# A hybrid eight-layer kernel: the begin of relative attention in another order, projections and adapter products inside the ends of its calls

## The reference

```python
# relative attention, 16 heads of 8
qx, kx, vx = split_head(x @ Wq.T), split_head(x @ Wk.T), split_head(x @ Wv.T)
srel = srel_skew(jnp.einsum('bhnd,hmd->bhnm', qx, ex))       # ex: rel_embed by head
qk = (jnp.einsum('bhnd,bhmd->bhnm', qx, kx) + srel) * inv_dim
atten = jax.nn.softmax(qk - mask, axis=-1)                   # causal
out = jnp.einsum('bhnm,bhmd->bhnd', atten, vx)...
return out @ Wp.T + bp
# adapter layer: 8 experts of width 64, two chosen by sequence
gate = jax.nn.softmax(x.mean(axis=1) @ gate_w.T); top_w, top_i = top_k(gate, 2)
h = gelu(x @ Wd + bd) * top_w;  out = h @ Wu + top_w * bu
```

## Time and profile before

| | |
|---|---|
| median of the 3 timed runs | 3797.18 us (3792.64 to 3798.52) |
| the profiled execution, its own time | 3799.16 us |
| its span | 3797.1 us |
| TensorE busy | 3561.5 us, 94% |
| VectorE busy | 2288.1 us, 60% |
| ScalarE busy | 1731.8 us, 46% |
| GpSimd busy | 822.9 us, 22% |
| mean granted TensorE clock | 0.992 |

### The profile page before, as it was taken

How to read it: one execution, slowest core, us unless ns; L and a number is a source line. 1 busy time by engine, 2 the same in 40 slices (tenths; PEclk the granted TensorE clock), 3 DMA queues, 4 the chain that set the end, 5 groups by cost and what they waited for, 6 DMA issues and landing times.

```text
span 3797.1 us, 78536 instructions
## 1 busy us (share of the span) xinstructions
PE 3561.5 (94%) x31023; PEld 2402.4 (63%) x31023; DVE 2288.1 (60%) x7482; ACT 1731.8 (46%) x3542; POOL 822.9 (22%) x1374
## 2 busy tenths in 40 slices
PE   6999999988999999998899999998889999999888
PEld 3666667666565667766556556776665656677665
DVE  4546455677554655567755554567776555456766
ACT  2425333466442523356644252335565335233556
POOL 3202023411210302332021030333302112033330
PEclk8999999999999999999999999999999999999999
DMA  3000000000000000000000000000000000000000
GB/s 89 2 1 2 1 1 1 2 2 2 13 1 1 2 1 1 1 2 2 1 13 1 1 2 1 1 1 2 2 7 8 1 1 1 1 1 1 2 2 9
DMA packets 27032, 17.47 MB, mean 5 GB/s; under 512 B 9425, under 2 KB 26274, under 8 KB 26658
## 3 DMA queue, kind: packets, MB, share of 16 engines
q1 hardware_dynamic: 26658, 12.32, 1.2%
HBM read 10.22 MB, written 2.10 MB: 3 GB/s over the span
## 4 chain that ended last, share of the span: by engine, by line
PE 69%; DVE 11%; POOL 7%; ACT 6%; issue 5%; SPq 1%; DVEq 0%; another core or an unknown queue 0%; POOLq 0%
PE banks L1252 9%; PE banks L1219 8%; PE banks L1214 8%; PE banks L1064 5%; PE banks L1103 5%; POOL work L563 5%; PE banks L1118 4%; PE banks L1043 3%; PE banks L1306 3%; PE banks L1538 3%; ACT work L887 2%; ACT work L881 2%; PE banks L1373 2%; PE banks L1551 2%; DVE work L2034 2%
## 5 line engine op out<-in xcount | busy, mean ns | idle before, releaser
L1723 DVE CUSTOM_DVE_ANT_0 work<-banks,mask_row 128x512 f32<-128x512 f32 (+3 forms) x1024 | 433.9, 486 | 276.1 <-PE banks L1064 276.0
L718 ACT ACTIVATE work<-banks 128x512 f32<-128x512 f32 x352 | 209.3, 597 | 654.1 <-PE banks L1214 638.9
L1814 DVE TENSOR_TENSOR work<-work,banks 128x512 f32<-128x512 f32 x352 | 242.0, 688 | 426.5 <-PE banks L1219 404.6
L519 POOL TENSOR_TENSOR rstd<-rstd,half 128x4 f32<-128x4 f32 x65 | 65.6, 1009 | 1933.9 <-DVE rstd L1647 1933.9
L741 ACT ACTIVATE work<-banks 128x384 f32<-128x384 f32 (+1 forms) x768 | 358.8, 534 | 255.2 <-PE banks L1103 254.7
L1103 PE MATMUL banks<-work 32*128 32x512 f32 (+3 forms) x2048 | 443.8, 464 | 6.5 <-DVE work L1723 3.9
L1252 PEld LDWEIGHTS banks<-wd,work 128*128 128x128 f32 (+2 forms) x4096 | 355.0, 189 | 135.3 <-issue 131.4
L1064 PE MATMUL banks<-work 32*128 32x384 f32 (+3 forms) x2048 | 406.1, 457 | 11.9 <-ACT work L727 6.4
L1252 PE MATMUL banks<-wd,work 128*128 128x128 f32 (+2 forms) x4096 | 365.8, 278 | 0.0
L530 POOL TENSOR_SCALAR_AFFINE_SELECT work<-work 128x128 f32<-128x128 f32 (+1 forms) x768 | 253.4, 333 | 460.8 <-ACT work L741 437.5
L1103 PEld LDWEIGHTS banks<-work 32*128 32x128 f32 x2048 | 243.0, 183 | 77.2 <-ACT work L741 39.4
(11 more groups left out here) (320 smaller groups left out, 6596.6 us busy)
## 6 DMA issues: line engine op xcount, KB each, us to landing
x_a<-in_L_attn_a_x_dram SPq DMA_DIRECT2D x5, 256.0 KB, 2.8
x_b<-in_L_attn_a_x_dram SPq DMA_DIRECT2D x4, 256.0 KB, 3.0
wg<-in_L_ffn_Wg_dram SPq DMA_DIRECT2D x2, 512.0 KB
wu<-in_L_ffn_Wu_dram SPq DMA_DIRECT2D x2, 512.0 KB
wd<-in_L_ffn_Wd_dram SPq DMA_DIRECT2D x16, 64.0 KB
out_dram<-x_a SPq DMA_DIRECT2D x4, 256.0 KB, 2.5
out_dram<-x_b SPq DMA_DIRECT2D x4, 256.0 KB, 2.6
wk_l<-in_L_attn_a_Wk_dram SPq DMA_DIRECT2D x1, 512.0 KB, 4.1
```

The costliest lines, as they stand in the source:

```text
L1723: m = eng.tensor_tensor_reduce(out=summed[:, k % 2, col:col + N], in0=bank(bk)[:, col:col + N], in1=mask_row[:, T - N:T], scale=1.0, scala ...
```

## The change

Nothing is added to or taken from what is computed; two fill products fewer are issued in a turn. It has six edits.

1. The rest of q goes to `xn` of the same sequence (free by then), the rest of k to its own place (`res_k`), so the buffer of mask step 0 no longer overlaps them. VectorE's order becomes: rest of q, mask(0) high, rest of k, mask(0) middle, low of q, low of k, values, mask(1), and both copies of stacked k.
2. GpSimd's mask(1) waits for VectorE's two instructions of mask(0) (`r_qm`) in place of both low parts.
3. TensorE does round 0 of the relative products before the first two spreads; these and round 1 follow, behind a wait for the values.
4. b's projection, and ScalarE's high parts for it, move from the start of b's relative call into the end of a's, behind the last `weigh`; the output transposes go to bank 6. a's sum into x on VectorE moves behind b's low parts.
5. The third adapter call's gate product (bank 3) and four down products move into the end of b's relative call, around the last head group and in the place of the two fills of `pe_out`.
6. In the adapters the gate product stands behind two tiles of up products instead of three; before the relative calls `pe_norm` stands behind two tiles of the second call's instead of four. The first sums of scores wait for the selects of their own blocks instead of for all of them.

```diff
@@ part(...) of relative attention
-        res, at = part(ring_at, [2, T])
-        k_parts, at = part(at, [3, T], BF16)
+        k_parts, _ = part(ring_at + 2 * T, [3, T], BF16)
+        res_k, _ = part(ring_at + 2 * T + 3 * T // 2, [T])
@@ pool_rel, mask(c)
                 if c == 1:
-                    eng.wait_ge(r_shift, n + 1)
-                    eng.wait_ge(a_lo, 2 * n + 2)
+                    eng.wait_ge(r_qm, 12 * n + 2)
@@ end of act_rel
-            if n == 1:
+            if n == 0:
+                act_first_parts(eng, 1, float(HD) ** -0.5)
+            else:
                 gate_exp(eng, 2)
@@ pe_adapters
-            up(n, (0, 1, 2))
+            up(n, (0, 1))
             eng.wait_ge(xnT_ok, adapter_call(n + 1))
             gate_products(eng, n + 1, 7)
-            up(n, (3,))
+            up(n, (2, 3))
...
-            up(n + 1, (0, 1, 2, 3))
+            up(n + 1, (0, 1))
+            if n == 0:
+                pe_norm(eng, adapter_call(n + 1) + 1, 0)
+            up(n + 1, (2, 3))
@@ pe_rel, begin
             eng.wait_ge(a_res, 2 * n + 2)
-            eng.wait_ge(a_v, 4 + n + 1)
-            pe_spread(eng, n, 0)
-            pe_spread(eng, n, 1)
             for i in range(P // 8):
+                if i == 1:
+                    eng.wait_ge(a_v, 4 + n + 1)
+                    pe_spread(eng, n, 0)
+                    pe_spread(eng, n, 1)
@@ pe_rel, end
             weigh(NG - 1)
-            if n == 1:
-                gate_products(eng, 2, 1)
-            group_rows(eng, n, NG * (5 + n) - 1, 7)
-            pe_out(eng, 4 + n, rel_call(n), w[:, 3, :], bp_row, 0, lambda: fill(eng, 3, 2))
+            if n == 0:
+                pe_project(eng, 1, w)
+            else:
+                gate_products(eng, 2, 3)
+                adapter_down(eng, 2, 0)
+            group_rows(eng, n, NG * (5 + n) - 1, 7)
+            if n == 1:
+                adapter_down(eng, 2, 1)
+                adapter_down(eng, 2, 2)
+            pe_out(eng, 4 + n, rel_call(n), w[:, 3, :], bp_row, 6,
+                   lambda: fill(eng, 3, 2) if n == 0 else adapter_down(eng, 2, 3))
@@ rel on VectorE, begin
+                first_rest(0)
+                eng.wait_ge(r_shift, n + 1)
+                mask_q(eng, 0, 0).then_inc(r_qm, 1)
+                first_rest(1)
+                eng.wait_ge(a_mid, 2 * n + 1)
+                mask_q(eng, 0, 1).then_inc(r_qm, 1)
+                last_part(0)
+                last_part(1)
+                if n == 1:
+                    add_to_x(4, a_y, 4)
+                eng.wait_ge(a_proj, 3 * n + 3)
+                copy_values(2)
+                eng.wait_ge(a_lo, 2 * n + 2)
+                mask(1)
                 stack_k(n, 0)
-                mask(1)
                 stack_k(n, 1)
...
-                eng.wait_ge(r_diag, 4 * (P // IC) * n + 4 * (P // IC))
...
+                    if p == 0:
+                        eng.wait_ge(r_diag, 4 * (P // IC) * (n + 1) - (3, 1, 0)[j])
```

More of the change, by code:

```diff
@@ L685, in act_norm, with rest, act_first_parts @@
             eng.activation(xnTs[j % 2][:, :], bank(bk), ACT.Copy).then_inc(xnT_ok, 1)
-        def act_parts(eng, n, scale):
+        def rest(n, w):
+            return (xns[n][:, :, :].rearrange("p t d -> p (t d)"), res_k)[w]
+        def act_first_parts(eng, n, scale):
             eng.wait_ge(a_proj, 3 * n + 1)
@@ L691, in act_parts @@
             eng.activation(qk_part(1, 0), bank(1), ACT.Copy).then_inc(a_hi, 1)
+        def act_parts(eng, n):
             for w in range(2):
                 eng.wait_ge(a_res, 2 * n + w + 1)
-                eng.activation(qk_part(w, 1), res[:, w, :], ACT.Copy).then_inc(a_mid, 1)
+                eng.activation(qk_part(w, 1), rest(n, w), ACT.Copy).then_inc(a_mid, 1)
         def act_stack(eng, n, w, at):
@@ L1419, in gate_products, with adapter_down @@
             eng.matmul(bank(bk)[:, 0:E], gates[n // 2]["rep"], gateT[:, :], start=True, stop=True).then_inc(d_gate_ok, 1)
+        def adapter_down(eng, m, k):
+            if k == 0:
+                eng.wait_ge(xnT_ok, adapter_call(m))
+            if m == 2 and k == 3:
+                eng.wait_ge(d_lgs, m + 1)
+            eng.matmul(bank(k), downT[:, k, :], xnTs[m % 2][:, :], start=True, stop=True).then_inc(d_dn, 1)
         def pe_adapters(eng, n):
             def down(m):
-                eng.wait_ge(xnT_ok, adapter_call(m))
                 for k in range(KD):
-                    if m == 2 and k == 1:
-                        eng.wait_ge(d_lgs, m + 1)
-                    eng.matmul(bank(k), downT[:, k, :], xnTs[m % 2][:, :], start=True, stop=True).then_inc(d_dn, 1)
+                    adapter_down(eng, m, k)
             def mix_column(m):
@@ L1447, in up @@
                     i.then_inc(d_y, 1)
-            down(n)
+            if n == 0:
+                down(n)
             mix_column(n)
@@ L1667, in copy_values @@
                    .then_inc(a_v, 1)
-            def parts_of_qk(n, scale):
-                for w in range(2):
-                    eng.wait_ge(a_hi, 2 * n + w + 1)
-                    eng.scalar_tensor_tensor(out=res[:, w, :], in0=bank(w), scalar=(scale, 1.0)[w],
-                                             in1=qk_part(w, 0), op0=ALU.mult,
-                                             op1=ALU.subtract).then_inc(a_res, 1)
-                eng.memset(q_parts[:, 0:2, 0:1], 0.0).then_inc(r_shift, 1)
-                for w in range(2):
-                    eng.wait_ge(a_res, 2 * n + w + 1)
-                    eng.wait_ge(a_mid, 2 * n + w + 1)
-                    eng.tensor_tensor(qk_part(w, 2), res[:, w, :], qk_part(w, 1),
-                                      ALU.subtract).then_inc(a_lo, 1)
-                eng.wait_ge(a_proj, 3 * n + 3)
-                copy_values(2)
             def stack_k(n, at):
@@ L1998, in rel, with first_rest, last_part @@
             def rel(n):
-                parts_of_qk(n, float(HD) ** -0.5)
+                def first_rest(w):
+                    eng.wait_ge(a_hi, 2 * n + w + 1)
+                    eng.scalar_tensor_tensor(out=rest(n, w), in0=bank(w), scalar=(float(HD) ** -0.5, 1.0)[w],
+                                             in1=qk_part(w, 0), op0=ALU.mult,
+                                             op1=ALU.subtract).then_inc(a_res, 1)
+                def last_part(w):
+                    eng.wait_ge(a_res, 2 * n + w + 1)
+                    eng.wait_ge(a_mid, 2 * n + w + 1)
+                    eng.tensor_tensor(qk_part(w, 2), rest(n, w), qk_part(w, 1),
+                                      ALU.subtract).then_inc(a_lo, 1)
                 def mask(c):
-                    if c == 0:
-                        eng.wait_ge(r_shift, n + 1)
-                        eng.wait_ge(a_lo, 2 * n + 2)
                     if c >= 2:
```

23 lines of the change are left out of this document (15 added, 8 removed).

## The result

| | before | changed |
|---|---|---|
| median of the runs | 3792.2 us (12 runs, 3786.7 to 3800.4) | 3803.6 us (12 runs, 3797.6 to 3811.0) |
| ratio, 95% interval | | 1.0030 (1.0022 to 1.0039) |
| span of the profiled execution | 3797.1 us | 3804.4 us |
| mean granted clock | 0.992 | 0.988 |

The changed kernel is **slower by 0.3%**; 3793.5 us and "the same" had been forecast, with a range up to 3800. Both intervals lie above 1, so the change makes the kernel slower; by how much, 0.1 or 0.3%, differs between the two series.

What follows compares the result with a forecast made beforehand. TensorE (69% of the chain) was taken as the bound, GpSimd as second limit in the loop. +0.1 - 0.8 - 0.26 = -0.95 us a turn, -3.8 us in four, gave 3795.4, as median 3793.5 us; range 3776 to 3800.

Steps and rivals of the forecast that it cites:

- Adapters into a's call: Adapter calls ahead of a's relative call: the norm two tiles before the end starts a's projection 0.8 us earlier.
- Begin of a's call: Reordered steps before a's selects: low part of k held up beside GpSimd's mask, selects 0.65 us later.
- the higher of two bounds: Low part of k on VectorE beside GpSimd's mask(1): between 0.6 and 2.6 us, taken as 2.6.
- Loop's end: End of a's loop follows GpSimd's chain, 0.65 us later, less 0.58 us of TensorE idle time: +0.1 us.
- the split wait: Loop's end: first sum goes after the first of the last four selects, 1.4 us sooner, removing 0.58 us TensorE idle.
- b's call: b's relative call: selects 0.55 us earlier and 0.23 us of idle time gone, -0.8 us.
- End of b's call: Into the third adapter call: early down products gain nothing and cost 0.7 us; gate product 0.26 us sooner.
- Sum without the clock: Whole kernel: -0.95 us a turn, -3.8 us over four turns.
- rival 3: Three new TensorE idle stretches a turn could drop its clock, 1.7 us each; all 12 give 3814 us; chance 0.08.
- one counterexample: End of a turn, TensorE waiting for rows of xn_a: 1.56 us idle left the clock at full, cited against rival 3.
- Rival 1: Begin of both relative calls: low part of k isn't held up, values 2.0 us earlier, -4.8 us a turn, 3778; chance 0.17.
- Rival 2: Loop: GpSimd's chain has slack and the end follows TensorE, -2.3 us a turn, 3788 us; chance 0.12.

Runs made afterwards that it cites:

- e3: Changed kernel with one wait more: GpSimd's mask(1) waits for both low parts again, early down products left in; 3781.6 us, ratio 0.9961 to before.
- e2: Changed kernel with 15 fills instead of 6 in front of the third adapter norm; 3792.6 us, ratio 0.9991 to before.
- r2: Changed kernel with 11 fills instead of 6 in front of the third adapter norm; 3791.7 us, ratio 0.9989 to before.
- r1: Changed kernel run once more, unedited, for a second trace; 3799.3 us, ratio 1.0011 to before.
- e5: Changed kernel with 8 fills instead of 6 in front of the third adapter norm; 3799.6 us, ratio 1.0012 to before.
- e6: Kernel before with only the adapter calls' new order (gate product one tile ahead, norm of a's call two tiles ahead); 3785.6 us, ratio 0.9980.
- e4: Changed kernel with down products back behind b's output projection and GpSimd's mask(1) waiting for both low parts; 3774.4 us, ratio 0.9945 to before.
- e8: e4 with rounds 0 and 1 both ahead of the first spreads; 3768.2 us, ratio 0.9931 to before.
- e1: Changed kernel with the third adapter call's down products back behind b's output projection, gate product still early; 3782.5 us, ratio 0.9966 to before.
- e7: e4 with b's projection put back at the begin of b's call; 3779.3 us, ratio 0.9961 to before.

## Why the prediction was wrong

By its own steps:

- **Adapters into a's call**, -0.8 us: measured -0.86 us. Right.
- **Begin of a's call.** The low part of k at 2.6 us, the higher of two bounds: 2.52 us. TensorE idle 1.99 us in front of the spreads (2.3 forecast). Selects 14.35 us after the projection forecast, 14.23 us measured. The rule of the Trainium skill, SBUF — State Buffer, section "Who interferes with whom", by which the higher bound was to hold, agrees here: where the two engines overlap, whichever instruction started second is held up. The low part of q started first and took its 0.69 us, GpSimd's mask then took 2.42 instead of 2.03 us, and the low part of k, behind it, 2.52 us; in e3, with nothing beside it, 0.69 us.
- **Loop's end.** +0.1 us for a's call forecast; it is 1.34 - 0.86 - 0.67 = -0.19 us. The stage behind the first scores, where the split wait was to gain 0.58 us, is 0.67 us shorter (no run isolates that wait), and the selects were later by 0.44 us, not 0.65 us.
- **b's call**, -0.8 us: -0.95 - 0.31 = -1.26 us.
- **End of b's call.** The early down products delay x_b and gain nothing: rows of `xn_b` 10.16 us after the last weigh instead of 9.12 us, TensorE idle 1.98 us (2.1 forecast). With the clock at full (e2, r2) the gate product comes at 14.56 us, 0.09 us sooner than before, for 0.26 us forecast.
- **Sum without the clock**: -3.8 us forecast, -6.2 us by the table. e2 and r2, the changed kernel with its clock held behind the norm, ran 2.0 and 3.1 us under before. That this is near the forecast is partly luck: the stages gained more than forecast, and some 3 us went by the clock in b's calls.

**The step that failed is rival 3's weight: the sum priced the clock behind the new gap in front of the third adapter norm at nothing.** It cost 9.3 us in the first trace and 10.6 us in r1's. In r1 that is the whole miss: 4.6 us over before instead of 3.8 us under it, 8.4 us off, with 2.4 us more gained in the stages than forecast. In the first series, 15 us off, it is the larger part; the rest lies in clock falls elsewhere and in the ends of the turns, whose cause stays open.

The prediction named the gap, its place and its length, and then set the clock aside with one counterexample: "1.56 us of idle time at 1912.5 left the clock at full". That was another place. Before keeps the clock there in all four turns (1.56, 1.56, 1.43 and 1.13 us idle), so more rows of that place would not have helped. e5 made a gap of 1.55 us at the place in question, and the clock fell in three turns of four. Nor is a short gap safe: in turns 2 and 4 of e6 the clock fell 2 us behind a gap of 0.91 us, a few microseconds ahead of the old place; in turns 1 and 3 it did not. Turn 2:

```profile
1902.74 1.12 PE L1439 MATMUL banks<-up_b,work 8*128 8x128 f32 x8 [0.91 <-ACT work L847]
...
1904.00:1908.00 4.00, 4.00 (x24) 4.00 (x24) 1.16 (x10) 0.00 (x0) 0.00 (x0) 0.61 0.22 66
```

A rule of the Trainium skill spoke for the rival (TensorE: Matmul & The Clock Gate, section "Part 1: The HAM clock gate": slow is the default and activity lifts it), and it was given 0.08. The rival itself was half right. Of its 12 stretches the four in front of the third adapter norm lost the clock, 8 times in 8 over two traces. The eight in front of the spreads kept it in both traces, all but one in r1 (1.99 us idle in a's calls, 1.18 us in b's). Its price of 1.7 us per stretch was too low for this place: 1.5 us once and 2.5 to 2.8 us in the other seven turns, since most of the way from the norm to the gate product lies in the slow stretch. The point from which it decides, seven stretches, was too high for the same reason: four turned a gain of 6.2 us into a loss of 3 to 4 us by the stages.

Rival 1 fell with the 2520 ns. e3 built what it described and gained 1.85 and 1.35 us a call, where it had forecast 2.0 us. Rival 2 fell too, for the changed kernel: its first scores follow the selects (28.0 us, as in e4) and not round 2 on TensorE. But TensorE's own bound was close. e8, which takes 3.5 us out in front of GpSimd's chain, gains 0.46 us, and then TensorE bounds the loop.

## What to carry to other kernels

- Work moved ahead of a dependent chain on another engine can cost twice: it delays that chain, and it no longer covers it. Here the down products were the cover for VectorE's sum, statistics and norm; moved forward, they opened a 2 us gap that had not been there. Before you move TensorE work, ask what it was hiding.
- A gap that the schedule opens on TensorE has two prices, its length and the clock behind it. If the next thing on the path is TensorE work, assume that the clock falls, unless the same place with the same gap is seen to keep it in every turn; rows from elsewhere prove nothing. Here fills that covered all but 0.91 us of it did as well as fills that covered it whole, and gave 8 us.
- When two engines lock each other out, let the shorter instruction on the critical path go first, and let the other engine collide with something that nobody waits for: one wait more gave e3 12.8 us by the stages. (Its median is 22 us under the first series of the changed kernel and 18 us under the second; of the rest, 3.7 to 5.0 us are smaller clock losses behind the norm.)

## What the runs showed of the hardware

- Whether an idle time of TensorE drops its clock is not a matter of length alone. In front of the third adapter norm 1.98 us lost it in 12 turns of 12 (the changed kernel, r1, e3), 1.55 us in 3 of 4, and 0.91 us in none of 4. In front of a's spreads 1.99 us (2.2 us in traces that lack the record of the first spread product) lost it in 2 of 24 calls (the six traces that have this gap: the changed kernel, r1, e1, e2, e5, r2), once each in r1 and e5. What sets the two places apart, no run shows.
- Where the clock falls in untouched code differs from version to version. e7, with 10.3 us more work on the path by its stages, was only 4.9 us slower than e4; in its trace two stretches of some 600 us, the first of them without an edited layer, ran at a clock of 0.99 and 1.00 instead of 0.98 and 0.99. Why is not shown. So differences of up to some 5 us (0.13%) between two versions of this kernel can come from where the clock falls elsewhere, and the comparison by stages is the safer one.
- GpSimd's mask takes 2.42 us when it starts during VectorE's low part of q, and 2.04 us when it starts first (e3), while the VectorE instruction behind it is held to 2.52 us (low part of k) and 2.75 us (mask). The copy of values out of PSUM overlaps the same mask and takes its 0.68 us (e3).
